# Transposing graph 0's activations on TensorE in the prologue of a two-layer graph attention kernel

## The chip, the cores and the metric

The kernel runs on one core of a Trainium2 chip. The metric is the device time of one launch in microseconds (us), the median of several runs.

## The reference

Sixteen graphs of 512 nodes with 256 features each. Every graph passes through two layers of single-head masked attention with a layer norm, and then through one layer of eight-head masked attention with a layer norm:

```python
for k in range(2):                      # "L0", layers 0 and 1
    q = x @ Wq[k].T + bq[k];  kk = x @ Wk[k].T + bk[k]          # 512 x 128
    scores = where(adj == 0, -1e10, q @ kk.T / sqrt(128))
    attn = where(adj == 0, 0, softmax(scores))
    x = layer_norm(x + (attn @ x) @ Wc[k].T, ln_g[k], ln_b[k])
q, k, v = x @ Wq + bq, x @ Wk + bk, x @ Wv + bv                 # "L1", 8 heads of 32
scores = where(adj == 0, -inf, q_h @ k_h.T / sqrt(32))
out = layer_norm((softmax(scores) @ v_h) @ Wo + bo + x, gamma, beta)
```

## The kernel before

**Tiles and slots.** A tile is 128 rows of a 512 x 512 score matrix; four tiles are a slot. An `L` slot is one layer of the first kind for one graph, an `H` slot is one head of the last layer. For a tile, TensorE makes scores into `ps_s` (`scores`), VectorE adds the mask and takes the row maximum (`mask`, line 1066), ScalarE exponentiates (`exp`, line 970), TensorE transposes the 128 x 512 probabilities in four parts (`transposes`, line 806), and ScalarE or VectorE copies them out of `ps_t` (lines 976, 1073). In an `L` slot VectorE then makes the low half of the pair (`low_tile`, line 1101). Which of the four copies VectorE does is in `PRO_COPIES`, `LOOP_COPIES` and `TAIL_COPIES`: `(3,)` means the fourth.

**Pairs.** Operands of the products are pairs of 16-bit values, a high part and the rest (low). A product of pairs is three matmuls (`split_product`, line 793). So each operand that comes out of PSUM costs one ScalarE instruction (high) and one VectorE instruction (low).

**Jobs.** Everything else is a job, in two halves where not said otherwise: `QK` (q and k of an `L` layer), `XW` (x times Wc), `AV` (attention times XW in four parts, then residual and statistics), `N` (normalization, after a power on GpSimd, `rstd_of`, line 608), `QH` and `V` (q, k and v of the last layer), `M` (a mask from the adjacency), `W` (a layer's weights scaled by the previous layer norm's gain and split: high on ScalarE as half 0, line 992, low on VectorE as half 1, line 1113), `D`, `B` and `C` (the shift of the layer norms sent through the weights to the biases; `B` makes all of them in one job of fp32 matmuls, lines 825, 817, 835 and 837, most with one column), `S` (the first weights). The jobs share three PSUM banks, `ps_j`; the pair of numbers in a row names the banks, and a job waits in `bank` until the one before it in that bank has been read.

**The order.** Each engine walks the same list. The prologue is four blocks in `PRO_BLOCKS`: block 0 has layer 0 of graphs 0 and 1, block 1 layer 1 of graph 0, block 2 layer 1 of graph 1, block 3 the heads 0 to 2 of graph 0. A block's first list of jobs is done ahead of its tiles; in the second list the last element says behind which tile's transposes TensorE does each part. VectorE and ScalarE do the work that belongs to it one tile later (`late_jobs`, so that a job's part may lie behind another tile's copy on these engines), in the order tile, row, part; at the last tile of a block both lists come together. All engines are in order. After the prologue the loop body (`LOOP_SLOTS`, `LOOP_JOBS`: ten slots) runs 14 times and a tail ends the program.

**Transposed activations.** `QK`, `XW`, `QH` and `V` need x transposed. GpSimd splits x or a layer's normalized rows `y_l` into a pair (`split`, lines 623 and 626: a cast and a subtraction; for graph 0's x VectorE does the subtraction, line 1128), and a DMA in SyncE's queue turns the pair (`turn_x` into `xt`, `turn_x2` into `xt2`). GpSimd then applies gain and shift for the residual (lines 613 and 617). SyncE's queue also holds every load and, in `stack_parts`, the path of the heads' q and k through DRAM: four `bounce` stores and sixteen `stack` loads, without which the `H` scores can't start (`stacked`).

## Time and profile before

| | us |
|---|---|
| median of 3 runs | 1213.43 (1211.64 to 1213.87) |
| the profiled execution | 1213.54 |
| its span, first to last instruction | 1211.8 |

| engine | busy, share of the span |
|---|---|
| TensorE | 1155.4 us, 95% |
| VectorE | 989.3 us, 82% |
| ScalarE | 923.2 us, 76% |
| GpSimd | 538.9 us, 44% |

The profile is one execution. PE is TensorE's matmuls, PEld its weight loads, DVE is VectorE, ACT ScalarE, POOL GpSimd, SPq SyncE's queue. "Idle before" an instruction is put down to the work that came last before it; "issue" is an idle time that the profile puts down to nothing.
### The profile page before, as it was taken

What the parts mean: (1) busy time and instruction counts of PE and PEld (TensorE: products, weight loads), DVE (VectorE), ACT (ScalarE), POOL (GpSimd) and SP (SyncE); (2) the same over time, 40 slices, a digit from 0 to 9 for tenths busy, and PEclk for the clock granted to TensorE, in tenths of its full rate; (3) what the DMA queues carried; (4) which work ended last, traced back from release to release, by engine and by line L of the source; (5) the groups of instructions that cost most, each with busy time, mean ns of one, the idle gap of its engine ahead of it and who ended that gap; (6) DMA issues with size and microseconds to landing.
All of it is one profiled execution on the core that took longest, in us unless ns stands there. A gap on an engine that the chain in (4) does not pass through costs nothing.

```text
span 1211.8 us, 28408 instructions
## 1 busy us (share of the span) xinstructions
PE 1155.4 (95%) x9572; PEld 840.7 (69%) x9572; DVE 989.3 (82%) x2680; ACT 923.2 (76%) x2112; POOL 538.9 (44%) x400
## 2 busy tenths in 40 slices
PE   5977999999999999999999999999999999999796
PEld 2754677777777777777777777777777777777463
DVE  4676789888888988888898888889888888988676
ACT  3235887878878787887878788787878888787774
POOL 1452344453464345346434534644453464444330
PEclk9799999999999999999999999999999999999999
DMA  8116161442615243251514325161442617132311
GB/s 242 36 36 153 23 176 36 124 90 71 153 36 167 45 122 88 67 161 36 172 39 123 89 81 146 36 177 34 125 91 78 145 37 179 32 76 79 95 33 36
DMA packets 170687, 114.06 MB, mean 94 GB/s; under 512 B 107184, under 2 KB 152240, under 8 KB 170544
## 3 DMA queue, kind: packets, MB, share of 16 engines
q1 hardware_dynamic: 168384, 104.37, 33.9%
q0 software_dynamic: 2160, 7.87, 1.9%
q8 instruction: 79, 1.29, 0.4%
q14 instruction: 64, 0.52, 0.1%
HBM read 61.87 MB, written 25.17 MB: 72 GB/s over the span
## 4 chain that ended last, share of the span: by engine, by line
PE 74%; DVE 11%; ACT 7%; issue 5%; DMA 2%; POOL 1%; DVEq 0%; POOLq 0%; SPq 0%; ACTq 0%
PE ps_j L793 32%; PE ps_t L806 18%; PE ps_j L910 9%; PE ps_s L779 6%; PE ps_s L785 6%; ACT probs L970 3%; ACT pt_l L976 2%; DVE some_l L1203 2%; DVE masked_s L1066 2%; DVE y_l L1217 2%; DMA xt<-ys 1%; PE ps_j L918 1%; DVE xw L1196 1%; DVE stats_L L1086 1%; DVE pt_l L1101 1%
## 5 line engine op out<-in xcount | busy, mean ns | idle before, releaser
L1066 DVE CUSTOM_DVE_ANT_0 masked_s<-ps_s,mask 128x512 f32<-128x512 f32 x640 | 424.4, 680 | 16.3 <-PE ps_s L785 14.5
L970 ACT ACTIVATE probs<-masked_s,nm_h 128x512 f32<-128x512 f32 x512 | 367.2, 718 | 88.6 <-DVE nm_h L1066 82.3
L806 PE MATMUL ps_t<-ident,probs 128*128 128x128 f32 x2560 | 391.4, 276 | 11.7 <-ACT pt_h L976 6.0
L806 PEld LDWEIGHTS ps_t<-ident,probs 128*128 128x128 f32 x2560 | 305.2, 142 | 93.9 <-issue 31.1
L976 ACT ACTIVATE pt_h<-ps_t 128x512 f32<-128x512 f32 x404 | 237.7, 588 | 64.5 <-PE ps_t L806 61.7
L785 PE MATMUL ps_s<-stack 128*128 128x512 f16 x512 | 194.7, 381 | 4.3 <-DVE nm_h L1066 3.8
L793 PE MATMUL ps_j<-xw,pt_l 128*128 128x256 f16 x1536 | 189.4, 275 | 0.0
L793 PEld LDWEIGHTS ps_j<-xw,pt_l 128*128 128x128 f16 x1536 | 151.4, 99 | 31.1 <-issue 0.5
L608 POOL TENSOR_TENSOR rstd_L<-var_eps_L,minus_half 128x4 f32<-128x4 f32 x32 | 32.8, 1025 | 264.8 <-DVE var_eps_L L1096 264.8
L910 PE MATMUL ps_j<-pt_h,v 128*32 128x256 f32 x2048 | 123.6, 382 | 2.2 <-DVE pt_h L1073 1.9
L1101 DVE TENSOR_TENSOR pt_l<-ps_t,pt_l 128x512 f16<-128x512 f32 x128 | 88.3, 690 | 37.6 <-ACT pt_l L976 28.4
L793 PE MATMUL ps_j<-xt,wq 128*128 128x512 f16 x384 | 94.9, 384 | 18.0 <-DMA xt<-xs 11.8
L970 ACT ACTIVATE probs<-masked_s,nm_l 128x512 f32<-128x512 f32 x128 | 91.9, 718 | 21.4 <-DVE nm_l L1066 21.2
L976 ACT ACTIVATE pt_l<-ps_t 128x512 f16<-128x512 f32 x124 | 73.6, 593 | 41.8 <-PE ps_t L806 38.0
L608 POOL TENSOR_TENSOR rstd_F<-var_eps_F,minus_half 128x4 f32<-128x4 f32 x16 | 16.3, 1019 | 192.5 <-DVE var_eps_F L1096 192.5
L793 PE MATMUL ps_j<-wc,xt 128*128 128x256 f16 x768 | 97.6, 273 | 3.2 <-DVE qt L1192 2.7
L779 PE MATMUL ps_s<-kt,qt 128*128 128x512 f16 x372 | 99.6, 379 | 0.2
L910 PEld LDWEIGHTS ps_j<-pt_h,v 128*32 128x32 f32 x2048 | 60.5, 109 | 54.8 <-issue 12.2
L970 ACT ACTIVATION_READ_ACCUMULATOR probs<-masked_s,nm_h 128x1 f32 x512 | 98.1, 192 | 0.0
L1073 DVE COPY pt_h<-ps_t 128x512 f32<-128x512 f32 x108 | 74.3, 688 | 27.1 <-PE ps_t L806 26.9
L793 PE MATMUL ps_j<-xt,wk 128*128 128x512 f16 x384 | 94.9, 384 | 0.0
L793 PEld LDWEIGHTS ps_j<-wc,xt 128*128 128x128 f16 x768 | 75.0, 98 | 23.7 <-issue 3.7
(123 smaller groups left out, 1647.6 us busy)
## 6 DMA issues: line engine op xcount, KB each, us to landing
stack<-bounce SPq DMA_DIRECT2D x256, 128.0 KB, 3.1
bounce<-parts SPq DMA_DIRECT2D x64, 256.0 KB, 2.7
adj_t<-adj_dram SPq DMA_DIRECT2D x30, 512.0 KB, 5.4
x<-x_dram SPq DMA_DIRECT2D x16, 512.0 KB, 4.0
out_dram<-y_f POOLq DMA_DIRECT2D x15, 512.0 KB, 3.4
stack<-adj_dram SPq DMA_DIRECT2D x2, 512.0 KB, 5.6
pt_h<-l_wc SPq DMA_DIRECT2D x2, 256.0 KB, 4.3
xt<-ys SPq DMA_TRANSPOSE x32, 4.4
```

Source lines behind the costliest of these rows:

```text
L608: pool.tensor_tensor(rstd[s][:], var_eps[s][:], minus_half[:], ALU.pow).then_inc(rstd_ready[s], 1)
L779: last = pe.matmul(dst, q_t[:, a, r * P:(r + 1) * P], k_t[:, c], start=n_ == 0, stop=n_ == 2)
L785: pe.matmul(dst, stack[:, n, 0, r * P:(r + 1) * P], stack[:, n, 1, :], start=True, stop=True).then_inc(scores_done, 1)
L793: last = pe.matmul(dst, lhs(a, e), rhs(c, e), start=n == 0, stop=n == len(terms) - 1 and not more)
L806: last = pe.transpose(ps_t[r % 2][:, t], probs[:, r, t * P:(t + 1) * P], ident[:])
L910: last = pe.matmul(out_bank[h * HD:(h + 1) * HD, 2 * r * P:2 * (r + 1) * P], v1[:, b % 2, t, col:col + HD], pt_of(b, 4 * g + h)[:, t, 2 * ...
L970: act.activation(probs[:, r], masked_s[:, r], ACT.Exp, bias=nm[:, n, r:r + 1], scale=-1.0, accum_out=total[:, n, r:r + 1]).then_inc(exps, 1)
L976: act.activation(dst, ps_t[r % 2][:], ACT.Copy).then_inc(copied_act, 1)
L1066: dve.tensor_tensor_reduce(out=masked_s[:, r], in0=ps_s[scores_bank(pos)][:], in1=m[:, r], scale=-scale, scalar=NONE_LEFT, op0=ALU.add, op ...
L1073: dve.tensor_copy(dst, ps_t[r % 2][:]).then_inc(copied_dve, 1)
L1101: dve.tensor_tensor(dst, full, high, ALU.subtract).then_inc(ready, 1)
L1203: dve.tensor_scalar(some_l[:], sum_l[:, l_buffer(b, l)], SUM_FLOOR, None, ALU.max).then_inc(some_ready, 1)
```

## The change

- A new job `X`: TensorE transposes graph 0's x, and `y_l` after each of its two layers, four 128 x 128 fp32 transposes for each half; ScalarE writes the high part from PSUM, VectorE the low part. `turn_x(0, 0)`, `turn_x(0, 1)` and `turn_x2(0)` leave SyncE's queue, and GpSimd no longer splits for graph 0. `X` stands first in block 0, behind the eighth tile of block 0, and in the first list of block 2. Graph 1 onwards is turned by DMA as before, with renumbered waits.
- `B` is cut in two: it keeps the sums for the second `L` layer, and a new job `Z`, behind tile 1 of block 1, makes those for the last layer (28 of its instructions).
- The low half of `W` for layer 1 moves from tile 2 to tile 5 of block 0; `W` for the last layer moves from tile 0 of block 1 to tiles 5 and 6 of block 0.
- In block 2 `QH` moves from tile 3 to tiles 0 and 1; `V` and half of `AV` for graph 1 move from there into block 3, `M` for graph 2 and `C` move too. The bank numbers are dealt anew.
- In the three `H` slots of block 3 VectorE copies two of four tiles instead of one.

```diff
@@ -55,34 +55,36 @@
...
     (3, [("L", 0, 0), ("L", 0, 1)],
-     [("S", None, 0, 0), ("QK", (0, 1), 0, 0), ("XW", (2, 0), 0, 0)],
+     [("X", (0, 1), 0, 0), ("S", None, 0, 0), ("QK", (2, 0), 0, 0), ("XW", (1, 2), 0, 0)],
      [("D", None, 0, 0, (1,)),
-      ("QK", (1, 2), 1, 0, (0, 0)),
+      ("QK", (0, 1), 1, 0, (0, 0)),
       ("M", None, 1, 0, (0,)),
       ("N", None, 0, 0, (4,)),
-      ("AV", (0, 1), 0, 0, (2, 2, 3, 3)),
-      ("AV", (0, 2), 1, 0, (6, 7, 7, 7)),
-      ("XW", (2, 0), 1, 0, (3, 4)),
-      ("B", (1, 2), 0, 0, (5,)),
-      ("W", None, 0, 1, (2, 2)),
+      ("AV", (2, 0), 0, 0, (2, 2, 3, 3)),
+      ("X", (1, 0), 0, 1, (7, 7)),
+      ("AV", (2, 1), 1, 0, (6, 7, 7, 7)),
+      ("XW", (1, 2), 1, 0, (3, 4)),
+      ("B", (0, 1), 0, 0, (5,)),
+      ("W", None, 0, 1, (2, 5)),
+      ("W", None, 0, 2, (5, 6)),
       ("M", None, 1, 1, (0,)),
       ("N", None, 1, 0, (7,))]),
     (3, [("L", 1, 0)],
-     [("QK", (2, 0), 0, 1), ("XW", (1, 2), 0, 1)],
-     [("W", None, 0, 2, (0, 0)),
+     [("QK", (0, 2), 0, 1), ("XW", (0, 1), 0, 1)],
+     [("Z", (2,), 0, 0, (1,)),
       ("AV", (0, 1), 0, 1, (2, 3, 3, 3)),
...
       ("N", None, 0, 1, (3,))]),
     (3, [("L", 1, 1)],
-     [("QK", (2, 0), 1, 1), ("XW", (1, 2), 1, 1)],
-     [("C", (0,), 0, 0, (1,)),
-      ("M", None, 2, 0, (1,)),
-      ("QH", (0, 1), 0, 0, (3, 3)),
-      ("QH", (1, 2), 0, 1, (3, 3)),
-      ("V", (1, 2), 0, 0, (3, 3)),
-      ("AV", (1, 2), 1, 1, (3, 3, None, None))]),
+     [("QK", (2, 0), 1, 1), ("XW", (1, 2), 1, 1), ("X", (0, 1), 0, 2)],
+     [("QH", (2, 0), 0, 0, (0, 0)),
+      ("QH", (1, 2), 0, 1, (1, 1)),
+      ("C", (0,), 0, 0, (2,))]),
     (4, [("H", 0, 0), ("H", 1, 0), ("H", 2, 0)],
      [],
-     [("M", None, 2, 1, (5,))]),
+     [("V", (0, 2), 0, 0, (1, 3)),
+      ("M", None, 2, 0, (3,)),
+      ("M", None, 2, 1, (5,)),
+      ("AV", (1, 2), 1, 1, (6, 8, None, None))]),
...
-PARTS = {"AV": 4, "OG": 3, "R": 1, "N": 1, "S": 1, "B": 1, "C": 1, "D": 1, "M": 1}
+PARTS = {"AV": 4, "OG": 3, "R": 1, "N": 1, "S": 1, "B": 1, "Z": 1, "C": 1, "D": 1, "M": 1}
...
-PRO_COPIES, TAIL_COPIES = [(3,)] * PRO_SLOTS, [(3,)] * 5 + [(1, 3)] * 8
+PRO_COPIES, TAIL_COPIES = [(3,)] * (PRO_SLOTS - 3) + [(1, 3)] * 3, [(3,)] * 5 + [(1, 3)] * 8
...
+        def dma_turn(b, l):
+
+            return (None, 1)[b] + l if b < 2 else nth(b, l) - 1
+
+        def wait_xt(eng, b, l):
+
+            if b == 0:
+                eng.wait_ge(x_lo, 2 * (l + 1))
+            else:
+                eng.wait_ge(xt_in, 16 * dma_turn(b, l))
+
+        def wait_xt2(eng, b):
+
+            if b == 0:
+                eng.wait_ge(x_lo, 6)
+            else:
+                eng.wait_ge(xt2_in, 16 * b)
+
+        def x_parts(l, half):
+
+            return [xt2[:, a, half] if l == 2 else xt[:, l_buffer(0, l), a, half] for a in range(2)]
+
...
                 L = nth(b, l)
                 if l == 0:
-                    sp.wait_ge(xs_ready, b + 1)
+                    sp.wait_ge(xs_ready, b)
                 else:
-                    sp.wait_ge(ys_ready, nth(b, 0) + 1)
+                    sp.wait_ge(ys_ready, dma_turn(b, 0))
                 settle(sp)
...
-                if not early(L, 1):
-                    sp.wait_ge(xt_in, 16 * L)
+                if dma_turn(b, l) > 1:
+                    sp.wait_ge(xt_in, 16 * (dma_turn(b, l) - 1))
...
-            turn_x(0, 0)
...
-            turn_x(0, 1)
...
-            turn_x2(0)
...
-                if not early(b, 1):
-                    pool.wait_ge(xt_in, 16 * (nth(b - 1, 0) + 1))
+                if not early(b, 2):
+                    pool.wait_ge(xt_in, 16 * dma_turn(b - 1, 0))
                     settle(pool)
-                split(x_tile(b), xs, xs_hi, None if early(b, 1) else xs_ready, b)
+                split(x_tile(b), xs, xs_hi, xs_ready, b - 1)
...
-                if l == 0 and early(b, 2):
-                    if b == 1:
-                        pool.wait_ge(xt_in, 16 * (nth(0, 1) + 1))
-                        settle(pool)
-                elif l == 1 and early(b, 1):
-                    pool.wait_ge(xt_in, 16 * (nth(1, 1) + 1))
+                if b == 0:
+                    return
+                if b > 1:
+                    pool.wait_ge(xt2_in, 16 * (b - 1))
                     settle(pool)
-                else:
-                    pool.wait_ge(xt2_in, 16 * b)
+                if l == 1:
+                    pool.wait_ge(xt_in, 16 * dma_turn(b, 1))
                     settle(pool)
-                    if l == 1:
-                        pool.wait_ge(xt_in, 16 * (nth(b, 1) + 1))
-                        settle(pool)
-                split(y_l, ys, ys_hi, ys_ready, nth(b, l))
...
-            split_x(0)
...
+                    if name == "Z":
+                        pe.wait_ge(head_bias_ready, 1)
+                    if name == "X":
+                        pe.wait_ge(x_lo, 2 * l + half + 1)
...
+                def shift_through(sums, n, w, c0, shift_n):
+                    for c in range(DC):
+                        last = pe.matmul(sums[:, n:n + 1], w(c)[:, c0:c0 + P],
+                                         shift_c[:, shift_n, c:c + 1], start=c == 0, stop=c == DC - 1)
+                    return last
+
+                if name == "X":
+                    if half == 0:
+                        if l == 0:
+                            pe.wait_ge(x_in, 16)
+                        else:
+                            pe.wait_ge(normed["L"], nth(0, l - 1) + 1)
+                    out_bank = bank(banks[half], before)
+                    for t in range(NT):
+                        last = pe.transpose(out_bank[:, t * P:(t + 1) * P],
+                                            (y_l if l else x0)[:, t, half * P:(half + 1) * P], ident[:])
+                    last.then_inc(x_turned, 1)
                 if name == "B":
...
@@ -825,18 +856,22 @@
                         pe.matmul(wide[:, 0:D], shift_wide[:, 0, c], raw["wc0"][:, (DC + c) * D:(DC + c + 1) * D],
                                   start=c == 0, stop=c == DC - 1)
                     for n, raw_n in enumerate(("wq0", "wk0")):
-                        shift_through(n, lambda c: raw[raw_n][:, (DC + c) * F:(DC + c + 1) * F], 0, 0)
+                        last = shift_through(sums, n, lambda c: raw[raw_n][:, (DC + c) * F:(DC + c + 1) * F], 0, 0)
+                    last.then_inc(bias_sums, 1)
+                if name == "Z":
+
+                    sums = bank(banks[0], before)
                     for n, raw_n in enumerate(("wq1", "wk1")):
                         for g in range(DC):
-                            shift_through(2 + 2 * n + g, lambda c: raw[raw_n][:, c * D:(c + 1) * D], g * P, 1)
+                            shift_through(sums, 2 * n + g, lambda c: raw[raw_n][:, c * D:(c + 1) * D], g * P, 1)
                     pe.wait_ge(biases_in, 16 * N_BIASES_IN)
                     for g in range(DC):
                         for c in range(DC):
-                            pe.matmul(sums[:, 6 + g:7 + g], raw["wv1"][:, c * D + g * P:c * D + (g + 1) * P],
+                            pe.matmul(sums[:, 4 + g:5 + g], raw["wv1"][:, c * D + g * P:c * D + (g + 1) * P],
                                       shift_c[:, 1, c:c + 1], start=c == 0, stop=False)
-                        last = pe.matmul(sums[:, 6 + g:7 + g], bv1[0:1, g * P:(g + 1) * P], ident[0:1, 0:1],
+                        last = pe.matmul(sums[:, 4 + g:5 + g], bv1[0:1, g * P:(g + 1) * P], ident[0:1, 0:1],
                                          start=False, stop=True)
-                    last.then_inc(bias_sums, 1)
+                    last.then_inc(head_sums, 1)
                 if name == "C":
 
...
-                    pe.wait_ge(xt_in, 16 * (L + 1))
+                    wait_xt(pe, b, l)
...
-                    pe.wait_ge(xt2_in, 16 * (b + 1))
+                    wait_xt2(pe, b)
...
-                if banks is None or name in "BC":
+                if banks is None or name in "BCZ":
                     return
                 bank = ps_j[banks[half % 2]][:]
+                if name == "X":
+                    act.wait_ge(x_turned, 2 * l + half + 1)
+                    act.activation(x_parts(l, half)[0], bank, ACT.Copy).then_inc(x_hi, 1)
                 if name == "QK":
...
+                    if early(b, 1):
+                        act.wait_ge(head_bias_ready, 1)
...
-                    dve.wait_ge(xs_hi, 1)
-                    dve.tensor_tensor(xs[:, 1], x0[:].rearrange("p t (c k) -> p c t k", c=DC), xs[:, 0], ALU.subtract)\
-                        .then_inc(xs_ready, 1)
...
-                    dve.wait_ge(biases_in, 16 * N_BIASES_IN)
                     dve.wait_ge(bias_sums, 1)
                     wide, sums = (ps_j[bank][:] for bank in banks)
                     dve.tensor_tensor(bq0[:, 1:2], bq0[:, 1:2], sums[:, 0:1], ALU.add)
-                    dve.tensor_tensor(bk0[:, 1:2], bk0[:, 1:2], sums[:, 1:2], ALU.add)
-                    dve.tensor_tensor(bq1[:], bq1[:], sums[:, 2:4], ALU.add)
-                    dve.tensor_tensor(bk1[:], bk1[:], sums[:, 4:6], ALU.add).then_inc(bias_added, 1)
+                    dve.tensor_tensor(bk0[:, 1:2], bk0[:, 1:2], sums[:, 1:2], ALU.add).then_inc(bias_added, 1)
                     dve.wait_ge(bias_added, 1)
-                    for bias in (bq0[:, 1:2], bk0[:, 1:2], bq1[:], bk1[:]):
+                    for bias in (bq0[:, 1:2], bk0[:, 1:2]):
                         dve.tensor_scalar(bias, bias, UP, None, ALU.mult)
-                    dve.tensor_copy(bv_wide[:], sums[:, 6:8].unsqueeze(2).to_broadcast([P, DC, P])).then_inc(bv_ready, 1)
                     dve.tensor_scalar(bx1[:], wide[:, 0:D], UP, None, ALU.mult).then_inc(bx1_hi, 1)
                     dve.wait_ge(bx1_hi, 1)
                     lower = slice(P // 2, P)
                     dve.scalar_tensor_tensor(bx1[lower], wide[lower, 0:D], UP, bx1[lower], ALU.mult, ALU.subtract)\
                         .then_inc(bias_ready, 1)
+                if name == "Z":
+                    dve.wait_ge(biases_in, 16 * N_BIASES_IN)
+                    dve.wait_ge(head_sums, 1)
+                    sums = ps_j[banks[0]]
+                    dve.tensor_tensor(bq1[:], bq1[:], sums[:, 0:2], ALU.add)
+                    dve.tensor_tensor(bk1[:], bk1[:], sums[:, 2:4], ALU.add).then_inc(head_added, 1)
+                    dve.tensor_copy(bv_wide[:], sums[:, 4:6].unsqueeze(2).to_broadcast([P, DC, P])).then_inc(bv_ready, 1)
+                    dve.wait_ge(head_added, 1)
+                    dve.tensor_scalar(bq1[:], bq1[:], UP, None, ALU.mult)
+                    dve.tensor_scalar(bk1[:], bk1[:], UP, None, ALU.mult).then_inc(head_bias_ready, 1)
...
-                if name in "SDBCWM":
+                if name in "SDBCZWM":
...
+                if name == "X":
+                    dve.wait_ge(x_hi, 2 * l + half + 1)
+                    hi, lo = x_parts(l, half)
+                    low_part(lo, bank, hi, x_lo)
```

## Rows read from the trace of the kernel before

**Rows 1.** Page part 5, one group (count, busy, mean ns).

```profile
L1066 DVE CUSTOM_DVE_ANT_0 masked_s<-ps_s,mask 128x512 f32<-128x512 f32 x640 | 424.4, 680 | 16.3 <-PE ps_s L785 14.5
```

**Rows 2.** Stretch of the loops: us, busy by engine (instructions), PEclk, DMA share, GB/s.

```profile
225.00:300.00 75.00, 74.84 (x637) 55.75 (x635) 64.67 (x176) 61.59 (x141) 34.19 (x25) 1.00 0.37 100
```

**Rows 3.** Timeline, start: start us, us, engine line op [idle before <- releaser].

```profile
4.80 1.04 POOL L623 CAST xs<-x 128x1024 f16<-128x1024 f32 x1 [3.29 <-DMA x<-x_dram]
...
8.05 0.69 DVE L1108 SCALAR_TENSOR_TENSOR wc<-pt_h,wc 128x512 f16<-128x512 f32 x1
...
11.78 2.72 PE L793 MATMUL ps_j<-xt,wq 128*128 128x512 f16 x6 [11.78 <-DMA xt<-xs]
```

**Rows 4.** Timeline, end of the first block.

```profile
39.65 0.87 DVE L1113 SCALAR_TENSOR_TENSOR wc<-pt_h,gain_up,wc 128x256 f16<-128x256 f32 x2
...
44.80 1.10 PE L825 MATMUL ps_j<-pt_h,rb 128*128 128x256 f32 x4 [2.22 <-issue]
...
45.74 4.42 PE L817 MATMUL ps_j<-shift_c,pt_h 128*128 128x1 f32 x24
...
47.11 0.68 DVE L1196 SCALAR_TENSOR_TENSOR xw<-ps_j,xw 128x512 f16<-128x512 f32 x1
...
50.56 2.34 POOL L613 TENSOR_TENSOR x<-y_l,gain 128x1024 f32<-128x1024 f32 x1
...
54.76 0.69 DVE L1101 TENSOR_TENSOR pt_l<-ps_t,pt_l 128x512 f16<-128x512 f32 x1 [6.96 <-ACT pt_l L976]
...
57.26 0.69 DVE L1073 CAST pt_l<-ps_t 128x512 f16<-128x512 f32 x1
...
61.12 0.88 DVE L1217 SCALAR_TENSOR_TENSOR y_l<-ps_j,r_l,x 128x256 f32<-128x256 f32 x2 [0.39 <-PE ps_j L793]
...
66.87 0.82 PE L793 MATMUL ps_j<-wc,xt 128*128 128x256 f16 x6 [0.45 <-issue]
...
68.40 1.89 PE L779 MATMUL ps_s<-kt,qt 128*128 128x512 f16 x8
```

**Rows 5.** Timeline, a weight low beside GpSimd; then all instructions of line 1095.

```profile
74.64 0.76 DVE L1113 SCALAR_TENSOR_TENSOR wq<-pt_h,gain_up,wq 128x256 f16<-128x256 f32 x1
...
73.00 2.13 POOL L626 TENSOR_TENSOR xs<-x,xs 128x1024 f16<-128x1024 f32 x1
...
L1095 DVE TENSOR_SCALAR minus_mean_L<-moments_L x32: 170/170/1208, 43.9 to 1123.4; 128x4 f32<-128x4 f32 x32
```

**Rows 6.** Stretches of 2 us, columns as in the second group.

```profile
42.00:44.00 2.00, 0.58 (x6) 0.34 (x4) 1.78 (x10) 1.09 (x3) 0.00 (x0) 1.00 0.00 0
...
46.00:48.00 2.00, 2.00 (x14) 2.00 (x13) 1.80 (x5) 0.15 (x2) 0.63 (x1) 0.62 0.00 0
...
54.00:56.00 2.00, 2.00 (x12) 1.42 (x10) 1.21 (x9) 0.60 (x1) 1.32 (x1) 0.50 0.90 200
...
86.00:88.00 2.00, 0.00 (x0) 0.00 (x0) 1.69 (x5) 0.39 (x1) 0.32 (x2) 1.00 0.00 0
```

**Rows 7.** Timeline, second block: wait for the fourth exponential.

```profile
77.05 0.66 PE L806 MATMUL ps_t<-ident,probs 128*128 128x128 f32 x4 [1.49 <-ACT probs L970]
```

**Rows 8.** Timeline, last two blocks of the prologue.

```profile
81.67 0.88 DVE L1217 SCALAR_TENSOR_TENSOR y_l<-ps_j,r_l,x 128x256 f32<-128x256 f32 x2
...
98.36 1.46 PE L793 MATMUL ps_j<-xt,wq 128*128 128x512 f16 x6 [1.05 <-DVE shift L1161]
...
101.87 0.75 DVE L1225 SCALAR_TENSOR_TENSOR parts<-ps_j,bk,parts 128x512 f16<-128x512 f32 x1 [0.54 <-ACT parts L1023]
...
108.50 2.78 PE L793 MATMUL ps_j<-xw,pt_l 128*128 128x256 f16 x24
...
111.11 0.81 PE L785 MATMUL ps_s<-stack 128*128 128x512 f16 x3
...
115.00 1.27 PE L806 MATMUL ps_t<-ident,probs 128*128 128x128 f32 x5
...
127.78 0.63 PE L806 MATMUL ps_t<-ident,probs 128*128 128x128 f32 x4 [0.34 <-ACT pt_h L976]
```

More of the change, by code:

```diff
@@ L502, in turn_x2 @@
             def turn_x2(b):
-                sp.wait_ge(ys_ready, nth(b, 1) + 1)
+                sp.wait_ge(ys_ready, dma_turn(b, 1))
                 settle(sp)
@@ L810, in job @@
                 L = nth(b, l)
+                def shift_through(sums, n, w, c0, shift_n):
[14 more added lines that the diff above has]
+                    last.then_inc(x_turned, 1)
                 if name == "B":
                     wide, sums = (ps_j[bank][:] for bank in banks)
-                    def shift_through(n, w, c0, shift_n):
-                        for c in range(DC):
-                            last = pe.matmul(sums[:, n:n + 1], w(c)[:, c0:c0 + P],
-                                             shift_c[:, shift_n, c:c + 1], start=c == 0, stop=c == DC - 1)
-                        return last
                     bank(banks[0], before)
```

7 lines of the change are left out of this document (5 added, 2 removed).

## Prediction

> **What bounds the kernel now.** I read the stretches first: in a stretch of the loops TensorE is busy for 74.84 of 75 us [rows 2], and the change touches nothing there. So the question is only when the loops begin: before, the first transposes of the loop stand at 127.78 [rows 8]. Next the timeline of the prologue, in order, asking at each gap of TensorE which wait ended last. Four places bind there. At the start TensorE waits 11.78 us for graph 0's x, split and turned [rows 3]. At the end of block 0 it makes the bias sums from 44.80, and VectorE, done with its work at 47.8, waits 6.96 us for what is queued behind them [rows 4]. In block 1 it waits 1.49 us for an exponential that stands behind the scaling of weights on ScalarE [rows 7]. And at the end the heads' first scores come at 111.11, their first transposes only at 115.00 [rows 8]. The execution took 1213.54 for a span of 1211.8, so 1.7 lies around the span; the median of the runs shown is 1213.43, the same within 0.1. A measurement of this kernel can tell about 0.2% (2.4 us) from no change. I write E for the end of graph 0's second AV (81.6, where the statistics begin at 81.67 [rows 8]).
>
> **Part 1, the start: -1.9 us.** x has landed by 4.8, where GpSimd takes it up [rows 3]. Instead of cast, subtraction and turn come eight transposes (four took 0.66 with a warm clock [rows 7]; up to twice that at the lower level), then a high and a low copy for each half; the low is at most the 0.69 of a low tile [rows 4]. The second half is ready at about 7.8. Then the weights bind: their last low ended at 8.74 [rows 3], and the X copies stand ahead of S on both engines and push it by some 0.6, to 9.3. GpSimd now takes graph 1's x at 8 to 9, beside these lows; part 2 shows what that can cost, and I add 0.6. First product at 9.9 instead of 11.78: -1.9. Bounds: 9.4 (-2.4), and 11.8 if a low has to wait for GpSimd's whole subtraction (2.13 for the same one later [rows 5]): 0. The adjacency loads move up in SyncE's queue past the removed turn; that only helps. Graph 1's turn is issued some 3 us earlier and is needed 2 us earlier, so it stays hidden. The turn for graph 0's layer 1 was hidden before; its removal gains nothing.
>
> **Part 2, the end of block 0: +3.2 us.** Without Z, B is 12 of its 40 instructions and takes 1.7 instead of 8.2 us (four in 1.10, and 8 of the 24 that took 4.42 [rows 4]). But behind B now stand, on VectorE, the low halves of two sets of weights and two X lows, and TensorE needs them: AV's third part for graph 1 goes into the bank of X, which is free only after the first X low. VectorE's chain, in times of before: free at 47.8 [rows 4]; low tile and B's small operations 2.5 (54.76 to 57.26 [rows 4]), less 0.6 for those that go to Z, to 49.7; W for layer 1 about 1.8 (its wider pair took 0.87, the two narrower ones less [rows 4]), to 51.5; copy and low of the eighth tile 1.4, to 52.9; W for the last layer, three such pairs without waits 2.4 to 2.6, to 55.4; the first X low at 56.0. So far AV's third part would start at 56.1 and the chain would come out even.
>
> To this comes GpSimd. It no longer splits for graph 0, so gain and shift, 2.34 each [rows 4], come right behind N, at 46.9 to 51.6 instead of from 50.56. That is when VectorE does B's scalings and W's lows. The trace shows what then happens: the weight low at 74.64 took 0.76, where two of its size took 0.87 together [rows 4], and GpSimd's subtraction from 73.00 ended at 75.13; of the 32 negated means, 0.17 in the median, the longest took 1.21 [rows 5]. Both end where GpSimd's operation ends. W's lows wait until 51.6, 1.9 to 2.3 us later than the chain above. I take 1.9: AV's third part at 58.0.
>
> The Trainium skill, "SBUF — State Buffer", section "SBUF: two separate sides", says that the two engines share a pair of ports under an exclusive lock, and that a VectorE instruction with two SBUF inputs blocks against a GpSimd one that reads SBUF, for the whole instruction. The trace agrees (0.76 for one against 0.87 for two). By the rule the sum has the full wait; if the two only slowed each other a little, the sum would be 1.9 lower.
>
> TensorE then has nothing from about 53 to 58. An idle time costs clock: after 42.6 to 44.8, almost idle, the granted clock fell to 0.5 in 46 to 48 and was still there in 54 to 56, with one-column products between; 86 to 88, wholly idle, was followed by no fall [rows 6]. Two of these twelve-matmul parts take 2.6 at full clock and 5.1 at half; I take halfway, and they end at 61.9 instead of 61.1. From the y at 61.12 to the second half of XW, which waited for q's low, it was 5.75, and 1.53 more to the scores at 68.40 [rows 4]. In the new banks the first half of XW also waits for q's low, so both halves lie behind it, 1.53 more: 61.9 + 5.75 + 3.06 = 70.7, +2.3. TensorE idles 3 us ahead of XW; half the price of a fall there adds 0.8 to 0.9. Together +3.2. Bounds: -0.9 (no wait, full clock) and +5.5 (the whole wait, half clock in both places).
>
> **Part 3, block 1: +1.9 us.** W is gone (the 1.49 wait and some 0.8 more of stop), Z has come behind tile 1. Z is 28 of the instructions that stood from about 47 to 53 at half clock, 5.9 us [rows 4, 6]; at full clock 3. So at best block 1 is 0.4 longer. One-column products were not enough to bring the clock back before [rows 6], so I expect a fall during or after Z, while 36 matmuls of AV, 3.9 at full clock, are on the path: a fall that covers 3 us of their work costs 1.5, +1.9. Bounds +0.4 and +4.0 (Z itself at half clock, and AV behind it).
>
> **Part 4, E to the heads' first transposes: -4.1 us.** Before: QH at 98.36 (E+16.7), last low of its k to 102.6 (E+21.0), scores at 111.11 (E+29.5), transposes at 115.00 (E+33.4) [rows 8]. Now: up to XW's second half nothing changes (E+8.6). X adds 0.9 on TensorE and puts two lows between XW's and the first mask, so this block's first transposes come at about E+12.7, 1.3 later than before. But QH stands right behind them, E+13.2. Its highs wait on ScalarE for the copy of tile 1, whose transposes stand behind QH (E+16.9), so k's low ends at E+19.0, 2.0 earlier. From there through DRAM it was at most 8.5 (102.6 to 111.11; TensorE was busy with V and AV until then, 2.78 each [rows 8]); I take 8.0: scores at E+27.0. TensorE has been idle since E+21.4. From scores to transposes it was 3.9, for VectorE first did AV's residual and statistics; these are gone from there, which leaves a mask (0.68 [rows 1]), an exponential and hand-overs, 2.2: E+29.2 or -4.2, less 0.1 for the clock. Bounds -5.0 and -2.0 (a fall in XW's wait, which before passed without one [rows 6]).
>
> **Part 5, the three H slots: +1.9 us.** Before, 115.00 to 127.78, 12.8 [rows 8], bound by ScalarE. Now V and half of AV come in, 5.6 of TensorE [rows 8], and VectorE has 12 masks and 6 copies at 0.61 to 0.69, two masks from adjacency (0.7 each) and one residual with statistics (2.1): 14.6 to 15.9; TensorE has 13.1, and 1.5 for the fall after its idle time. With some lead at the start I take 14.7: +1.9. Bounds +0.7 and +2.5.
>
> **Sum.** -1.9 + 3.2 + 1.9 - 4.1 + 1.9 = +1.0: a span of 1212.8, and 1214.5 us with the 1.7 around it.
>
> **The rivals.** *A: no change, the sum above* (within 2.4 of 1213.5; its own range 1211.1 to 1215.9), 0.38: the gains at both ends are paid back in the middle and by the longer H slots.
>
> *B, slower: TensorE's clock.* The change takes waits from TensorE but leaves it four idle stretches of 2.7 to 5 us (ahead of AV's third part, ahead of XW twice, ahead of the heads' scores) and one of one-column work. If each is followed by some us at half clock, as 42 to 44 was [rows 6], parts 2 and 3 stand near +4.5 and +3.0 and part 4 loses 0.6: +4, 1217.5. It decides from two more falls than the sum holds. Against it: the idle 86 to 88 had no fall. 0.32. The Trainium skill, "TensorE: Matmul & The Clock Gate", section "HAM oscillation — how this bites in real kernels", says that bursts separated by waits each start at the low clock and speaks against this layout; the rows bear it out after one of the two idle stretches shown. By it the time is B's.
>
> *C, faster: VectorE's chain is not held.* If W's lows slip in ahead of GpSimd's shift, part 2 is -0.9 to +0.5, the idle time ahead of AV's third part is under 3 us and the clock holds: about -4, 1209.5. For it: only 1.9 us of the chain hang on GpSimd, and VectorE idled 6.96 us there before. Against: GpSimd has its two operations queued back to back, while VectorE comes for the ports later. 0.30.
>
> Faster by over 0.2% 0.30, within 0.38, slower 0.32. The range, 1209 to 1219, reaches into both rivals and leaves out the ends of the bounds, where all go one way (-6 and +8).
>
> **What would show it.** Part 1: the first product at 9.4 to 10.5. Part 2: B under 2.5 us; weight lows over 0.6 beside GpSimd; AV's third part idle before it, put down to VectorE's X low or to "issue"; scores of block 1 at 68.40 - 1.9 + 3.2, about 69.7. Part 3: AV's end for graph 0 (E) at about 84.8. Part 4: H transposes at E+29. Part 5: the loops' first transposes at 128.8. It is wrong if the clock falls much oftener or less often, if VectorE's chain is short of the 10 us from 47.8 to 58, or if the path through DRAM lasts under 7 us.

## The result, and the profile after

The changed kernel takes 1220.82 us (median of 4 runs, 1219.65 to 1222.28), the kernel before 1213.65 beside it (4 runs, 1211.64 to 1214.51): a ratio of 1.0059, with a 95% interval of 1.0046 to 1.0071. It is slower, by 7.2 us. Forecast were 1214.5 and a range of 1209 to 1219, which leaves the time out.

The profiled execution took 1221.88 for a span of 1220.0, with a mean granted clock of 0.983 (before 0.990 in a span of 1211.8). The page's part 1 gives busy time, share of the span and instructions of each engine:

```profile
PE 1162.9 (95%) x9596; PEld 846.5 (69%) x9596; DVE 996.0 (82%) x2688; ACT 924.9 (76%) x2115; POOL 531.9 (44%) x395
```

The loops and the tail last as long as they did: GpSimd's first store of a result comes 8.2 us later than before (200.5, now 208.7), and the last stores in SyncE's queue end 8.2 us later too. So all of the loss is in the prologue. The timeline of TensorE there answers [rows 3], [rows 4] and [rows 8]:

```profile
9.67 2.72 PE L814 MATMUL ps_j<-xt,wq 128*128 128x512 f16 x6 [2.89 <-DVE wc L1148]
...
42.53 1.10 PE L856 MATMUL ps_j<-pt_h,rb 128*128 128x256 f32 x4 [2.10 <-issue]
43.47 0.95 PE L834 MATMUL ps_j<-shift_c,pt_h 128*128 128x1 f32 x8
...
56.26 5.25 PE L814 MATMUL ps_j<-xw,pt_l 128*128 128x256 f16 x24 [5.52 <-DVE xt L1141]
...
67.30 0.81 PE L814 MATMUL ps_j<-wc,xt 128*128 128x256 f16 x6 [3.19 <-issue]
...
72.02 3.01 PE L800 MATMUL ps_s<-kt,qt 128*128 128x512 f16 x12
...
76.25 1.84 PE L834 MATMUL ps_j<-shift_c,pt_h 128*128 128x1 f32 x16
...
81.35 2.77 PE L814 MATMUL ps_j<-xw,pt_l 128*128 128x256 f16 x12
...
84.76 4.34 PE L814 MATMUL ps_j<-xw,pt_l 128*128 128x256 f16 x36
...
95.97 1.44 PE L814 MATMUL ps_j<-wc,xt 128*128 128x256 f16 x6 [2.74 <-DVE qt L1239]
...
103.63 1.46 PE L814 MATMUL ps_j<-xt,wq 128*128 128x512 f16 x6
...
117.75 2.78 PE L806 MATMUL ps_s<-stack 128*128 128x512 f16 x5 [5.50 <-DMA stack<-bounce]
120.32 1.91 PE L827 MATMUL ps_t<-ident,probs 128*128 128x128 f32 x8
...
134.69 0.60 PE L827 MATMUL ps_t<-ident,probs 128*128 128x128 f32 x4
136.51 0.39 PE L806 MATMUL ps_s<-stack 128*128 128x512 f16 x1 [1.22 <-DVE nm_h L1106]
```

Read against the rows of before, step by step: the first product stands at 9.67 instead of 11.78 [rows 3], 2.1 us earlier. The first scores of block 1 stand at 72.02 instead of 68.40 [rows 4]: the lead has become a lag of 3.6. E, the y_l of graph 0's second AV, is at 89.14 instead of 81.67 [rows 8], a lag of 7.5; the heads' first transposes at 120.32 instead of 115.00, 5.3; the loops' first transposes at 134.69 instead of 127.78, 6.9; and the first QK of the loops at 140.66 instead of 132.39, 8.3.

The queues of VectorE and GpSimd between them, at the end of block 0:

```profile
45.11 2.35 POOL L636 TENSOR_TENSOR x<-y_l,gain 128x1024 f32<-128x1024 f32 x1 [2.08 <-DVE y_l L1217]
47.53 2.36 POOL L640 TENSOR_TENSOR x<-x,shift 128x1024 f32<-128x1024 f32 x1
...
46.11 0.69 DVE L1141 TENSOR_TENSOR pt_l<-ps_t,pt_l 128x512 f16<-128x512 f32 x1 [0.58 <-ACT pt_l L1011]
...
48.01 2.30 DVE L1153 SCALAR_TENSOR_TENSOR wq<-pt_h,gain_up,wq 128x128 f16<-128x128 f32 x2
50.23 0.60 DVE L1153 SCALAR_TENSOR_TENSOR wk<-pt_h,gain_up,wk 128x128 f16<-128x128 f32 x2
...
54.64 0.88 DVE L1153 SCALAR_TENSOR_TENSOR wv<-pt_h,gain_up,wv 128x256 f16<-128x256 f32 x2
55.43 1.28 DVE L1141 TENSOR_TENSOR xt<-ps_j,xt 128x512 f16<-128x512 f32 x2
```

The pair of weight lows that began at 48.01 took 2.30, the like pair behind it 0.60; it ended 0.4 us after GpSimd's shift, which ran from 47.53 to 49.89. The two lows of X are done by 56.7, and AV's third part, which waits for the first of them, begins at 56.26 after 5.52 us of idle TensorE.

Stretches of 2 us of the changed kernel, TensorE only (busy, instructions, granted clock, DMA share, GB/s), beside [rows 6]:

```profile
54.00:56.00 2.00, 0.00 (x0) 0.63 0.00 0
58.00:60.00 2.00, 2.00 (x11) 0.50 0.04 8
70.00:72.00 2.00, 2.00 (x13) 0.60 0.00 0
82.00:84.00 2.00, 2.00 (x11) 0.50 0.00 0
86.00:88.00 2.00, 2.00 (x21) 1.00 0.00 0
96.00:98.00 2.00, 2.00 (x10) 0.50 0.00 0
120.00:122.00 2.00, 2.00 (x9) 0.50 0.85 227
```

The granted clock is either 1 (2.4 GHz) or 0.5 (1.2 GHz); a value between is a stretch with both. Read in short stretches up to 145 us, TensorE of the kernel before is at half clock in 29.4 to 32.8, 46.5 to 56.7 and 114.8 to 118.2: 17.1 us. The changed kernel is in 27.2 to 30.6, 44.3 to 47.7, 54.5 to 61.4, 68.2 to 71.6, 78.4 to 85.3, 95.5 to 98.9 and 116.0 to 122.8: 34.1 us. All sums of half clock below are of these first 145 us; some 10 us more lie in the last 90 us of both kernels. They leave out the very start, where the trace prints 1.00 but the first six products took 2.72 us and the same kind later 1.46. Each of the four idle stretches that rival B named, and the one-column products of Z, has its fall.

### The profile page after: what moved, and what is told of

It is laid out like the page before. It is cut to its first block, busy times and chain, and to the rows that moved or that the text cites. A ratio compares the mean times of both kernels' runs of the same rounds, so it can differ in the third digit from the quotient of the medians.

```text
span 1220.0 us, 28456 instructions
## 1 busy us (share of the span) xinstructions
PE 1162.9 (95%) x9596; PEld 846.5 (69%) x9596; DVE 996.0 (82%) x2688; ACT 924.9 (76%) x2115; POOL 531.9 (44%) x395
## 4 chain that ended last, share of the span: by engine, by line
PE 77%; DVE 10%; ACT 6%; issue 4%; DMA 2%; POOL 1%; SPq 0%; DVEq 0%; POOLq 0%; ACTq 0%
PE ps_j L814 33%; PE ps_t L827 19%; PE ps_j L945 9%; PE ps_s L806 7%; PE ps_s L800 6%; ACT probs L1005 2%; DVE masked_s L1106 2%; DVE some_l L1250 2%; ACT pt_l L1011 2%; DVE y_l L1264 1%; PE ps_j L953 1%; DMA xt<-ys 1%; DVE xw L1243 1%; DVE pt_l L1141 1%; DVE stats_L L1126 1%
## 5 line engine op out<-in xcount | busy, mean ns | idle before, releaser
L814 PE MATMUL ps_j<-xw,pt_l 128*128 128x256 f16 x1536 | 193.4, 278 | 5.8 <-DVE xt L1141 5.5
L631 POOL TENSOR_TENSOR rstd_L<-var_eps_L,minus_half 128x4 f32<-128x4 f32 x32 | 32.8, 1025 | 262.9 <-DVE var_eps_L L1136 262.9
L814 PE MATMUL ps_j<-wc,xt 128*128 128x256 f16 x768 | 100.6, 277 | 5.9 <-issue 3.2
```

What stands on the lines that cost most here:

```text
L631: pool.tensor_tensor(rstd[s][:], var_eps[s][:], minus_half[:], ALU.pow).then_inc(rstd_ready[s], 1)
L814: last = pe.matmul(dst, lhs(a, e), rhs(c, e), start=n == 0, stop=n == len(terms) - 1 and not more)
```

## The experiments

All were timed beside the kernel before, whose median there was 1213.5 to 1213.7. The changed kernel was not timed again beside them: what is said against it goes by its 1220.82. Three theories stood after the result: *the clock* (the falls behind the idle stretches are the loss), *the queue* (VectorE, held by GpSimd and by two sets of weight lows, delays X's low, and what is idle in between is the loss itself), and *the split of the sums* (Z costs more on its own in block 1 than it took behind B).

**e1: GpSimd's shift after the weight lows.** One wait more on GpSimd:

```diff
                     pool.wait_ge(shift_ready, 1)
+                if norm == 0 and early(c, 1):
+                    pool.wait_ge(weights_ready, 3)
                 pool.tensor_tensor(dst[:], dst[:], h, ALU.add).then_inc(ln_done[s], 1)
```

> The changed kernel, but GpSimd adds the shift for graph 0's first layer only when VectorE has made all low halves of the weights. Theory of the shared port: the first low of W ran 47.9 to 50.2 because that addition stood from 47.53 to 49.89; without it the chain on VectorE is 1.9 us shorter, AV's third part starts at 54.4 instead of 56.26, and the time is 1219.0 (1220.8 less 1.9; 1217.5 if one fall of the clock goes with it). Rival, that the two only happened to coincide: no change, 1220.8.

Measured: 1217.88 (1212.66 to 1219.81, 10 runs), ratio 1.0033 [1.0019, 1.0047], 2.9 us less than the changed kernel. The first pair of lows is back to its own time, and AV's third part comes 1.7 earlier:

```profile
47.98 0.61 DVE L1155 SCALAR_TENSOR_TENSOR wq<-pt_h,gain_up,wq 128x128 f16<-128x128 f32 x2
...
54.54 4.45 PE L816 MATMUL ps_j<-xw,pt_l 128*128 128x256 f16 x24 [3.32 <-DVE xt L1143]
```

Half clock is 30.7 us in its profile instead of 34.1. GpSimd's hold on VectorE is real and costs some 2 to 3 us, the fall that goes with it included, but that is less than half of the loss.

**e4: the idle stretches filled.** The changed kernel, with products whose result is thrown away (128x512) ahead of AV's third part, of XW twice and of the heads' scores; nothing else moves.

```diff
+                    if (r, n) == (0, 0) and early(b, 1):
+                        warm(24)
...
+            def warm(n):
+                for _ in range(n):
+                    pe.matmul(ps_s[0][:], mean_64[:], wc0[:, 0, 0].rearrange("p c f -> p (c f)"),
+                              start=True, stop=True)
...
+                    if (b, l, r) == (1, 0, 2):
+                        warm(23)
...
+                    if (b, l, half) in ((0, 1, 0), (1, 1, 1)):
+                        warm(12)
```

> The changed kernel with idle TensorE kept busy: matmuls of 512 columns whose result is overwritten, 23 ahead of AV's third part for graph 1, 12 ahead of XW's first half in block 1 and of its second half in block 2, 24 ahead of the heads' first scores; each set is shorter than the idle time it stands in at full clock. Theory of the clock: the granted clock stays 1.00 behind each, AV's two parts take 2.6 instead of 5.2, XW 3.2 instead of 4.8, X and XW in block 2 1.5 less, the heads' start 1.5 less: 1214 to 1216. Rival, that VectorE and the path through DRAM set these ends anyway: 1220 to 1221.

Measured: 1213.55 (1209.75 to 1217.0, 10 runs), ratio 0.9998 [0.9981, 1.0015]. With 71 useless products more, the changed kernel is 7.3 us faster and stands level with the kernel before. TensorE around the first two of the four places:

```profile
52.44 5.13 PE L813 MATMUL ps_s<-wc,mean 128*128 128x512 f16 x23
57.41 2.78 PE L821 MATMUL ps_j<-xw,pt_l 128*128 128x256 f16 x24
...
62.62 2.75 PE L813 MATMUL ps_s<-wc,mean 128*128 128x512 f16 x12
65.93 0.83 PE L821 MATMUL ps_j<-wc,xt 128*128 128x256 f16 x6 [0.56 <-DVE qt L1250]
```

The 24 matmuls of AV take 2.78 instead of 5.25, although they begin no earlier (57.41), and XW's first products 0.83 with the rest at the same pace, so that the scores come at 68.99 instead of 72.02. The half-clock time in this profile is 17.1 us instead of 34.1. So 17.0 us less of half clock go with 7.3 us less in the medians, 0.43 us each (7.9 us less between the two profiled executions). With the order and all useful work as they were, the changed kernel stands where the kernel before stands: what it had lost against that one was clock. What makes the longest of these stretches is the queue of VectorE, as e2 shows next.

**e2: the weight lows back where they were.** W1's to tile 2 of block 0, W2's to the head of block 1:

```diff
-      ("W", None, 0, 1, (2, 5)),
-      ("W", None, 0, 2, (5, 6)),
+      ("W", None, 0, 1, (2, 2)),
...
-     [("Z", (2,), 0, 0, (1,)),
+     [("W", None, 0, 2, (0, 0)),
+      ("Z", (2,), 0, 0, (1,)),
```

> The changed kernel with both W jobs where they were before (low half for layer 1 at tile 2, the last layer's at tile 0 of block 1). Theory that the load moved onto VectorE at the end of block 0 is the loss: 6 us leave the chain there, AV's third part is not held, and block 1 takes back at most 2.3 us of it: 1216 to 1217. Rival, that TensorE's clock and Z are the loss: within 1 us of 1220.8.

Measured: 1210.77 (1206.18 to 1214.58, 10 runs), ratio 0.9973 [0.9956, 0.9991]: 10.0 us faster than the changed kernel, against 4 to 5 expected, and faster than the kernel before.

```profile
50.67 4.34 PE L814 MATMUL ps_j<-xw,pt_l 128*128 128x256 f16 x36
...
60.80 0.81 PE L814 MATMUL ps_j<-wc,xt 128*128 128x256 f16 x6 [3.20 <-issue]
...
68.08 1.84 PE L834 MATMUL ps_j<-shift_c,pt_h 128*128 128x1 f32 x16
...
73.69 4.09 PE L814 MATMUL ps_j<-xw,pt_l 128*128 128x256 f16 x36
...
105.02 2.77 PE L806 MATMUL ps_s<-stack 128*128 128x512 f16 x5 [5.51 <-DMA stack<-bounce]
```

AV's third part is not waited for at all: 36 matmuls of it and its neighbours run in one group of 4.34. I had counted 6 us of VectorE's chain less at most 2.3 in block 1. But here the falls behind the later stretches are gone as well, except the one before the heads' scores: XW's first half waited 3.20 as in the changed kernel (3.19) and ran at full clock. Half clock is 13.7 us. The mean clock of the ten runs is 0.9884 against 0.9835 in the changed kernel; by the slope given below, an estimate, that is 5.1 of the 10.0 us, which leaves the other half for the waiting itself. Why the same wait is followed by a fall in one kernel and not in the other no run here settles.

**e6: only W1's low back** (of e2's edit the line of W1, from tile 5 to tile 2; W2's low stays where the change put it).

> Only the low part of W1 goes back to tile 2 of block 0; W2's stays where the change put it (5, 6). It splits e2_weights_back, which moved both and was 10.0 us faster than the changed kernel. Theory: what held VectorE was its queue while GpSimd held the port, with W1's low (tile 5) and W2's low (tile 6) both standing ahead of the low part of X; either alone keeps part of the idle time ahead of AV's third part (3.3 us idle and a fall after it), so this gives about half, 1215 to 1217. Rival 1 (W1's low alone is the cost, because it stands beside GpSimd's shift): 1211 to 1212. Rival 2 (W2's low alone is the cost, because it stands right ahead of X's low): 1219 to 1221.

Measured: 1215.27 (1210.67 to 1217.76, 11 runs), ratio 1.0012 [1.0, 1.0024]. It is the half-way case of the theory: the idle time ahead of AV's third part is down to 1.62 (AV's third part at 54.66, waiting for the same low of X), and each of the two moves of weight lows costs about half of the 10 us (5.5 for W1's, the remaining 4.5 for W2's).

**e3: Z right behind B, at tile 5 of block 0**, as the sums stood before:

```diff
       ("B", (0, 1), 0, 0, (5,)),
+      ("Z", (2,), 0, 0, (5,)),
...
-     [("Z", (2,), 0, 0, (1,)),
-      ("AV", (0, 1), 0, 1, (2, 3, 3, 3)),
+     [("AV", (0, 1), 0, 1, (2, 3, 3, 3)),
```

> The changed kernel with Z right behind B (tile 5 of block 0) instead of behind tile 1 of block 1. Theory that the sums cost TensorE the same wherever they stand and that VectorE's chain of block 0 starts behind them: block 1 gains 4 to 6 us, block 0 loses 5 to 6, 1220 to 1222. Rival, that cutting the job in two is the loss: 1216.

Measured: 1220.15 (1217.45 to 1223.8, 10 runs), ratio 1.0049 [1.0035, 1.0063]. As expected, no different from the changed kernel within what these runs can tell: where Z stands only moves its price from block 1 to block 0 (scores of block 1 at 77.4, but E at 88.96 beside 89.14). So the place of Z is not the loss. Z was still a job of its own here, and what the cut itself costs was not tried.

**e7: the kernel before, filled in the same way**, ahead of its three stretches:

```diff
+                    if n_tile == 4:
+                        warm(12, dst)
...
                     bank(banks[0], before)
+                    warm(10, wide)
...
+                    if (b, l, half) == (1, 1, 1):
+                        warm(12, ps_s[0])
```

> The kernel before, with thrown-away products (128x512, about 0.22 us each) in three idle stretches: 12 ahead of the first scores of block 0's second slot (2.9 us idle), 10 ahead of the bias sums B (2.2 us idle), 12 ahead of XW's second half in block 2 (2.7 us idle). It asks what the change is worth with the clock held up on both sides: e4_warm against this. Theory (the falls follow idle stretches): the falls at 29 and at 46.5 go, 17.1 us at half clock become about 4, and the kernel gains 3 to 5 us: 1209 to 1210.5; the change then loses 3 us or more even without falls. Rival (the 28 one-column products of B bring the fall themselves, whatever stands ahead of them): half clock still from about 48 on, within 1.5 us of 1213.4.

Measured: 1212.65 (1210.5 to 1215.43, 11 runs), ratio 0.9996 [0.9987, 1.0005]: the rival's number. The stretches of its profile (columns as above) say why:

```profile
44.00:46.00 2.00, 2.00 (x6) 0.50 0.00 0
48.00:50.00 2.00, 2.00 (x20) 1.00 0.03 8
50.00:52.00 2.00, 2.00 (x13) 0.57 0.85 162
```

The ten products ahead of B ran at half clock for nearly all of their time (4.00 us for the ten, after 2.26 us idle), the clock was back at 48 to 50, and during the one-column products it fell once more. So B's fall does not hang on the idle time ahead of it alone, and the fillers could not save what they saved in e4. It also bounds what the comparison with e4 is worth: with fillers on both sides the change stands 0.9 us behind (1213.55 against 1212.65), inside what the two intervals leave open. That the change would lose 3 us or more even without falls, as the theory had it, did not come.

**e8: e2 with the old end of the prologue** (tables of blocks 2 and 3 and the copies as before the change; graph 0's x2 still turned by TensorE):

```diff
-      ("QH", (2, 0), 0, 0, (0, 0)),
-      ("QH", (1, 2), 0, 1, (1, 1)),
...
+      ("QH", (0, 1), 0, 0, (3, 3)),
+      ("QH", (1, 2), 0, 1, (3, 3)),
+      ("V", (1, 2), 0, 0, (3, 3)),
+      ("AV", (1, 2), 1, 1, (3, 3, None, None))]),
...
+PRO_COPIES, TAIL_COPIES = [(3,)] * PRO_SLOTS, [(3,)] * 5 + [(1, 3)] * 8
```

> e2_weights_back with the end of the prologue as before the change: blocks 2 and 3 have their old tables (QH and V at the last tile of block 2, AV's first two parts there too, C and M at tile 1) and the old split of the copies; graph 0's x2 is still turned by TensorE in block 2. Theory (of the prediction: the heads' earlier keys gain 4.1 us, ScalarE's and VectorE's work moved into the H slots takes 1.9 us and the loop's entry 1.4 us more): the old end costs about 1 us, 1211 to 1213. Rival (the moved work costs at least what the earlier scores bring): 1209 to 1210.8.

Measured: 1211.62 (1207.78 to 1217.02, 12 runs), ratio 0.9988 [0.9974, 1.0001]. 0.85 us more than e2, near the 1 us of the theory, but the two were not on the same chip, their intervals overlap and their runs spread over 8 us, so the sign is not shown. Its runs had the higher mean clock, 0.9909 against 0.9884, so at the same clock it would stand further behind e2.

**e5 and e10: e2 and fillers**, the best version: ahead of the first scores of block 0's second slot, of XW twice, and of the heads' scores.

```diff
+                    if n_tile == 4:
+                        warm(12, dst)
...
+                    if (r, n) == (0, 0) and early(b, 1):
+                        warm(24, dst)
...
+                    if (b, l, half) in ((0, 1, 0), (1, 1, 1)):
+                        warm(12, ps_s[0])
```

> The weights' low parts stand as before the change (as in e2_weights_back), and four idle stretches of TensorE are filled with products whose result is thrown away (128x512, fp16 operands, start and stop set, about 0.22 us each): 12 ahead of the first scores of the second slot of block 0, 12 ahead of the first half of XW in block 1 and of its second half in block 2, 24 ahead of the heads' first scores. e2_weights_back ran 1210.8 us and spent 13.7 us at half clock in the prologue. Theory (the loss is clock): with the idle stretches filled no fall is left at 28.5, 45.5 may stay, and the fall at 103.5 goes: some 7 to 10 us of half clock less. What that is worth is read from e4_warm, where 17 us less of it gave 7.3 us: 3 to 4 us, so 1207 to 1208. Rival (what remains of half clock lies beside VectorE and ScalarE, which set the pace there): within 1 us of 1210.8.

> The same kernel as e5_back_and_warm, on this call's chip, for the comparison with e9_av_two_tiles_earlier and for a second measurement of the fastest version: 1206 to 1209 if the first measurement (1207.43, six runs) was representative.

Measured: 1207.43 (1203.0 to 1209.47, 6 runs), ratio 0.9944 [0.9929, 0.996], and once more, as e10, 1207.25 (1204.39 to 1208.9, 6 runs), ratio 0.9944 [0.9931, 0.9958]: the theory's number twice. That is 6.2 and 6.5 us less than the kernel before beside it, and 13.4 less than the changed kernel. In the profile of e5, which is of its fastest execution, only 3.4 us at half clock are left, behind Z; in that of e10 it is 10.2. Ahead of the heads' scores:

```profile
96.82 5.34 PE L815 MATMUL ps_s<-wc,mean 128*128 128x512 f16 x24
102.36 0.82 PE L810 MATMUL ps_s<-stack 128*128 128x512 f16 x3 [0.20 <-DMA stack<-bounce]
...
104.57 1.36 PE L836 MATMUL ps_t<-ident,probs 128*128 128x128 f32 x8
```

Three scores take 0.82 there; in the changed kernel the first five took 2.78.

**e9: graph 1's second AV two tiles earlier** in the H slots of e5, against the 1.22 us that TensorE waits at the entry of the loops:

```diff
-      ("AV", (1, 2), 1, 1, (6, 8, None, None))]),
+      ("AV", (1, 2), 1, 1, (4, 6, None, None))]),
```

> e5_back_and_warm with the first two parts of graph 1's second AV two tiles earlier in the H slots (4 and 6 in place of 6 and 8). In e5_back_and_warm TensorE is idle for 1.22 us at the entry of the loops, because VectorE's y_l and row statistics of these parts stand ahead of a mask in its queue. Theory: earlier parts put that VectorE work where the third slot still has slack, and the 1.2 us come back: 1206.2 to 1206.8 beside 1207.4. Rival (VectorE has the same 2 us to do in the same slots and is the bound there wherever they stand): within 0.5 us of e10_back_and_warm_again.

Measured: 1210.62 (1207.36 to 1211.61, 8 runs), ratio 0.9975 [0.9965, 0.9986]: 3.4 us slower than e10 on the same chip. Neither theory had that. The wait went along with the work, grew from 1.22 to 1.87, and had a fall behind it (half clock from 118.3 to 121.7). Its profile is of its fastest execution, 0.75 us above that of e10, so it shows only part of the 3.4:

```profile
117.94 0.39 PE L810 MATMUL ps_s<-stack 128*128 128x512 f16 x1 [1.87 <-DVE nm_h L1117]
```

**All runs together.** Each run lists its own mean granted clock, so the clock can be read apart from the edits. Between runs of one and the same kernel (98 runs, those of the changed kernel and of e1 to e10, each against the mean of its own kernel) a mean clock higher by 0.001 goes with 1.04 us less. In 1210 us, 0.001 of the mean is 2.4 us at half clock, so that is 0.43 us each, as in e4. A correlation does not say by itself which of the two comes first; e4, where only the fillers differ, does. The four runs of the changed kernel average 0.9835, the 29 of the kernel before beside e5 to e8 0.9892: by that slope 5.9 us of the 7.2. e4 averages 0.9918, which by it is 8.6 us less than the changed kernel; 7.3 were measured.

**And the waits one by one.** In the profiles of the kernel before, the changed one, e1, e2, e3, e6 and e8 (no fillers in any), each wait of TensorE of over 2.7 us behind the first product, and whether half clock followed ("after" is the changed kernel):

| wait ahead of | us | falls behind it |
|---|---|---|
| first scores of block 0's second slot | 2.90 | 7 of 7 |
| XW's first half in block 1 | 3.19 to 3.20 | 3 of 6 (after, e1, e3) |
| XW's second half in block 2 | 2.74 to 2.75 | 2 of 7 (after, e1) |
| AV's third part, graph 1 (e1); AV behind Z (e3) | 3.32; 3.48 | e1; in e3 it was at half clock already |
| AV's third part, graph 1 (after); heads' first scores (after, e1, e2, e3, e6) | 5.50 to 5.65 | 6 of 6 |

## Why the prediction was wrong

The mechanisms of the sum stand in the trace; what failed is the size of one term that occurs in three parts, the price of the clock (taken at half a fall in parts 2 and 3 and at nothing for XW's wait in part 4, 5.4 to 5.7 us short together), and one term was missing, the entry of the loops (1.4).

**Part 1 was right.** 9.67 forecast as 9.9; the last weight low runs from 8.84 to 9.52, and GpSimd's cast, from 8.97, came too late to hold it, so the 0.6 added for it was not needed in this execution. In the profiles of e2, e4 and e6 the cast began first, the low was held, and the first product came at 10.5 to 10.65. In e2:

```profile
8.72 1.10 POOL L646 CAST xs<-x 128x1024 f16<-128x1024 f32 x1 [7.21 <-DMA x<-x_dram]
8.84 1.52 DVE L1148 SCALAR_TENSOR_TENSOR wc<-pt_h,wc 128x512 f16<-128x512 f32 x1
```

**Part 2: +5.7 instead of +3.2.** B takes 1.75 (42.53 to the transposes at 44.28), forecast 1.7. VectorE's chain is right almost to the tenth: AV's third part forecast at 58.0 in times of before, 56.1 with the lead of part 1, and it began at 56.26. So is the hold by GpSimd: 1.9 taken, 1.7 measured on the pair at 48.01 and once more as the 1.7 by which e1 begins earlier. The Trainium skill, "SBUF — State Buffer", section "SBUF: two separate sides", whose exclusive lock was cited there, agrees with 2.30 against 0.60. What was wrong are the two places where I took half a fall. AV's two parts took 5.1 at half clock, where I put halfway between 2.6 and 5.1: 1.3 short. XW, priced at half a fall (0.8 to 0.9), took 4.7 from 67.30 to the scores instead of 3.06: 0.8 short. The rest, 0.4, is the chain.

**Part 3: +3.9 instead of +1.9.** The fall came, as forecast, during Z, but it was twice as long: Z took 4.2 instead of 3 (3.4 at full clock in e2), and the clock stayed at half to 85.3, under AV's first twelve matmuls and the transposes on both sides of them; the other 36 took 4.34, 0.25 more than in e2. Without a fall the same block took 13.97 us from the first scores to E in e2 (63.85 to 77.82), 13.27 before the change (68.40 to 81.67) and 17.12 in the changed kernel (72.02 to 89.14): the layout costs 0.7, the clock 3.1, and the step had 1.5 for it. Up to Z the changed kernel and e2 take the same 4.23, so all of the 3.1 lies behind the start of Z. The step's best case, 0.4, was a slip: 3 for Z less the 2.3 for W is 0.7.

**Part 4: -2.2 instead of -4.1, by the clock alone.** Of its steps QH was forecast at E+13.2, scores at E+27.0, transposes at E+29.2. In the changed kernel they are at E+14.5, 28.6 and 31.2; XW's second half, 95.97, began after 2.74 us idle and ran at half clock. The same wait of 2.74 before had no fall behind it (the stretch 86 to 88 in [rows 6]), and from that one row I priced it at nothing. In e2, where XW ran at full clock and only the heads' fall is left, scores are at E+27.2 and transposes at E+29.8. In e5, with the clock held at both, E is at 75.37, QH at E+13.0, scores at E+27.0 and transposes at E+29.2. The path through DRAM was 8.2 (k's low ends at 109.57), forecast 8.0.

**Part 5 was right, and stopped too early.** 14.4 from the heads' first transposes to the loops', forecast 14.7. But the entry of the loops costs 1.4 more, which no part had. The first two parts of graph 1's second AV now stand at tiles 6 and 8, and the residual and statistics of both stand on VectorE ahead of a mask:

```profile
134.19 0.88 DVE L1264 SCALAR_TENSOR_TENSOR y_l<-ps_j,r_l,x 128x256 f32<-128x256 f32 x2
135.10 0.75 DVE L1126 BATCH_NORM_STATS2 stats_L<-y_l 128x6 f32<-128x256 f32 x2
135.77 0.68 DVE L1106 CUSTOM_DVE_ANT_0 masked_s<-ps_s,mask 128x512 f32<-128x512 f32 x1
```

TensorE waits 1.22 for it (136.51). I had counted this work (2.1 us there, 2.0 here with two small operations ahead of it, 133.79 to 135.77) against the length of the slots, and not asked which mask stands behind them and who waits for it.

Summed up: of the 7.2 us by which the span passed the forecast, 2.1 (part 2), 1.6 (part 3) and 1.7 to 2.0 (part 4) are clock, 5.4 to 5.7 together; 1.4 is the entry; the rest is what lies within the steps. Rival B was the right one, and too small: it had 4.5, 3.0 and 0.6 less gain for parts 2, 3 and 4, where 5.7, 3.9 and 2.0 came out, and it lacked the entry. A bound for everything going one way was in the text and was left out of the range. It was also added up wrong: the five upper bounds give +10.0 and the five lower ones -7.2, not +8 and -6, and the measured +8.2 lies between them. The falls may come together rather than one by one: after and e1 have falls behind all of their waits in the table, e3 behind the first XW only, e2, e6 and e8 behind neither. That they have a common cause is argued from this table, not shown; there is one profile of each kernel, and those of e6 and e8 are of executions 3.6 and 3.8 us below their medians.

What would have shown it beforehand: [rows 6] held one fall and one case without, and I took halfway. The kernel before has two stretches of this kind more, both with a fall, that were not among the rows: a wait of 2.90 ahead of 28.55 (half clock from 29.4 to 32.8) and one of 2.13 ahead of 114.05 (114.8 to 118.2). With them the count is three of four. (In e8 the second of these, 2.12 us ahead of 109.87, has no fall.)

The Trainium skill, "TensorE: Matmul & The Clock Gate", section "HAM oscillation — how this bites in real kernels", says of a kernel whose bursts of matmuls are separated by waits of some 3 to 5 us for a DMA that each burst starts at the low clock. In the changed kernel all six waits of over 2 us behind the first product (2.10 to 5.52) have a fall, but only three of the bursts begin in it (56.26, 95.97, 117.75); in the other three the clock falls 0.8 to 1.8 us after the first instruction. In e2 three of the five such waits have one (27.58, 43.83, 105.02, not 60.80 and 84.65). It was right as a warning, and the count varies.

## What to carry to other kernels

Where TensorE binds, read the granted clock next to every wait of two or more microseconds that a change makes or lengthens, and price the fall in full, at all places together, before giving any of it away: here between 5 and 6 of the 7 us lost were clock. Work that is only early by plan, such as a weight split with a late consumer, must not be put into a queue ahead of what TensorE waits for next; and a step moved past the end of a stage is followed to the mask or semaphore that stands behind it. If the idle time can't be avoided, discarded 128x512 products into a bank that is about to be overwritten can fill it: they kept the clock at all eight places of e4 and e5. Ahead of the one-column sums in e7 they did not.
